# One block in sixteen gets its product by C on VectorE, the others on GpSimd

## The reference

```python
def _L0_ffn_ref(x, A, B, W, bias):          # 64 arrows of rank 16, TOPK = 4
    vecs = jnp.einsum('arh,bsh->bsar', A, x)
    arrows = jnp.linalg.norm(vecs, axis=-1)
    _, idx = jax.lax.top_k(arrows, TOPK)
    routes = jax.nn.one_hot(idx, arrows.shape[-1], dtype=x.dtype).sum(-2) / TOPK
    v = jnp.einsum('bsa,bsar->bsr', routes, vecs)
    delta = jnp.einsum('bsa,ajr,bsr->bsj', routes, B, v)
    return jnp.einsum('bsh,jh->bsj', x, W) + bias + delta

def _L0_attn_ref(x, W_xproj, W_dt, b_dt, A_log, D_param):   # 16 states, rank 128
    xz = jnp.einsum('btd,rd->btr', x, W_xproj)
    delta_r, B_mat, C_mat = ...                              # xz cut in three
    delta = jax.nn.softplus(jnp.einsum('btr,dr->btd', delta_r, W_dt) + b_dt)
    dA = jnp.exp(delta[..., None] * -jnp.exp(A_log))
    Bu = delta[..., None] * B_mat[:, :, None, :] * x[..., None]
    # over time: h = dA_t * h + Bu_t;  y = sum(h * C_t[:, None, :], axis=-1)
    return y + x * D_param

x = x + 0.5 * _L0_ffn_ref(_layernorm(x), A, B, W, bias)
x = x + _L0_attn_ref(_layernorm(x), ...)
x = x + 0.5 * _L0_ffn_ref(_layernorm(x), A, B, W, bias)
```

## Time and profile before

| | |
|---|---|
| median of 3 runs | 2759.53 us (2757.13 to 2759.86) |
| profiled execution | 2758.88 us |
| its span, first to last instruction | 2757.1 us |
| granted TensorE clock, mean | 0.993 |
| PE busy | 94% of the span |
| POOL busy | 85% |
| DVE busy | 81% |
| ACT busy | 54% |

### The profile page before, as it was taken

The page is one execution under the profiler, slowest core; times in us unless marked ns, Lnnn a source line. Parts: engine busy times, 40 slices in busy tenths (PEclk is TensorE's granted clock), DMA queues, the critical chain, the costliest instruction groups (busy, mean ns, idle before and its releaser), DMA issues.

```text
span 2757.1 us, 39894 instructions
## 1 busy us (share of the span) xinstructions
PE 2586.1 (94%) x13593; PEld 1170.8 (42%) x13664; DVE 2219.7 (81%) x2933; ACT 1501.3 (54%) x3363; POOL 2349.9 (85%) x703
## 2 busy tenths in 40 slices
PE   4989999999999999999999999999999999899999
PEld 1444444444434444444444444444444444444444
DVE  7448888888888888888888888888888888888943
ACT  5346667665555655655556555565555555556511
POOL 1138999899989999999999999999999999999910
PEclk9999999999999999999999999999999999999999
DMA  5144544644464545554454445544455445454321
GB/s 217 55 116 152 151 137 141 179 146 139 143 166 143 154 127 155 154 150 143 144 169 137 143 143 170 155 149 133 146 170 151 157 128 156 141 146 153 92 62 54
DMA packets 333217, 390.29 MB, mean 142 GB/s; under 512 B 149459, under 2 KB 249939, under 8 KB 333014
## 3 DMA queue, kind: packets, MB, share of 16 engines
q1 hardware_dynamic: 316118, 354.18, 43.0%
q10 hardware_dynamic: 16896, 33.56, 4.1%
HBM read 250.82 MB, written 103.29 MB: 128 GB/s over the span
## 4 chain that ended last, share of the span: by engine, by line
PE 36%; DVE 34%; ACT 8%; DVEq 7%; issue 7%; DMA 4%; POOL 2%; ACTq 1%; SPq 0%; POOLq 0%
DVE mreg L1154 18%; PE pv L560 12%; PE po L560 7%; PE pv L564 6%; PE po L564 4%; ACT pA L940 3%; PE py L727 3%; DMA delta_scratch<-mreg 2%; DVE pv L1114 2%; DVE sel L1111 2%; DVEq L1119 2%; DVEq L1069 2%; DVE ln_st L1068 1%; DVEq L1113 1%; PE pv L689 1%
## 5 line engine op out<-in xcount | busy, mean ns | idle before, releaser
L528 POOL TENSOR_TENSOR mreg<-mreg 128x2048 f32<-128x2048 f32 x256 | 1161.8, 4538 | 96.8 <-ACT hst L926 92.5
L1154 DVE TENSOR_TENSOR_SCAN mreg<-pA,hst,mreg 128x512 f32<-128x512 f32 (+1 forms) x1024 | 1044.2, 1066 | 76.6 <-ACT pA L940 59.0
L940 ACT ACTIVATE pA<-mreg,nA 128x512 f32<-128x512 f32 (+1 forms) x1280 | 739.7, 597 | 398.3 <-DVE mreg L1154 372.0
L518 POOL TENSOR_TENSOR mreg<-mreg 128x1024 f32<-128x1024 f32 x340 | 794.9, 2362 | 122.3 <-DMA mreg<-delta_scratch 109.7
L560 PE MATMUL pv<-wA,xT 128*128 128x512 f16 x2016 | 458.1, 379 | 28.0 <-DVE xT L1091 26.5
L560 PE MATMUL po<-wW,xT 128*128 128x512 f16 x2016 | 469.6, 380 | 4.0 <-issue 0.5
L560 PE MATMUL po<-wB,uT 128*128 128x512 f16 x2016 | 465.8, 379 | 7.9 <-DVE xin L1077 7.4
L512 POOL TENSOR_TENSOR mreg<-mreg 128x2048 f32<-128x2048 f32 x86 | 389.5, 4529 | 5.5 <-issue 5.2
L560 PEld LDWEIGHTS pv<-wA,xT 128*128 128x128 f16 x2016 | 190.8, 98 | 305.9 <-ACT xT L847 65.8
L560 PEld LDWEIGHTS po<-wB,uT 128*128 128x128 f16 x2016 | 191.3, 98 | 266.3 <-issue 36.4
L560 PEld LDWEIGHTS po<-wW,xT 128*128 128x128 f16 x2016 | 196.0, 98 | 240.1 <-issue 26.3
(11 more groups left out here) (132 smaller groups left out, 2371.7 us busy)
## 6 DMA issues: line engine op xcount, KB each, us to landing
mreg<-delta_scratch SPq DMA_DIRECT2D x256, 512.0 KB, 5.2
mreg<-xnT_scratch SPq DMA_DIRECT2D x128, 256.0 KB, 4.9
delta_scratch<-mreg ACTq DMA_DIRECT2D x128, 256.0 KB
xin<-x SPq DMA_DIRECT2D x32, 512.0 KB, 4.2
x_scratch<-xin SPq DMA_DIRECT2D x32, 512.0 KB, 3.0
xnT_scratch<-auxs SPq DMA_DIRECT2D x32, 512.0 KB, 2.9
yT_scratch<-mreg SPq DMA_DIRECT2D x64, 256.0 KB, 5.6
uT<-yT_scratch SPq DMA_DIRECT2D x32, 512.0 KB, 5.2
```

Of the source, the lines that this page charges most:

```text
L518: pool.tensor_tensor(h[:, half * n:half * n + n, :], u, b.broadcast_to([P, n, c.width]), ALU.mult).then_inc(s_bm, 1)
L528: pool.tensor_tensor(h, h, by_c, ALU.mult).then_inc(s_cm, 1)
L940: last = nc.scalar.activation(dst[:, part, :], src[:, part, :], ACT.Exp, scale=nA[:, m:m + 1])
L1154: last = V.tensor_tensor_scan(h, split(pA[:, i % 2, :], c)[:, part, :], h, before, ALU.mult, ALU.add)
```

## The change

The constant GV = 3 names a group. In every tile the first block of group 3, block i with i % 16 == 12, no longer gets its product by C from GpSimd. VectorE scans that block out of Hr, but writes the states in place over the decays in PSUM (pA) instead of into Hr. After a drain and a wait for C's row it multiplies the states in pA by C's row and writes the product to Hr, where GpSimd's would have been, and gives s_sc behind that. GpSimd's product of group 3 covers the other three blocks. As the states of block 12 are then in pA alone, ScalarE copies their last column to hst from there (`keep_first`, with a drain), ahead of the decay of block 14, which overwrites the buffer. `keep_last` copies the columns of the other three blocks.

```diff
--- before.py
+++ after.py
@@ -11,6 +11,7 @@
 NPR = 3
 NXT = 3
 AHEAD = 10
+GV = 3
 LEAD = 14
 MIX_END = 48
 SCAN0 = 3
@@ -523,8 +524,9 @@
                 c = chunk_of_tile[G // 4]
                 pool.wait_ge(s_sv, G + 1)
                 pool.wait_ge(s_ldc[g], 16 * (c.q + 1))
-                h = split(Hr[:, G % NH, :, :].rearrange("p s t -> p (s t)"), c)
-                by_c = Cr[:, g, 0:c.width].unsqueeze(1).broadcast_to([P, 4 * c.parts, c.width])
+                first = c.parts if g == GV else 0
+                h = split(Hr[:, G % NH, :, :].rearrange("p s t -> p (s t)"), c)[:, first:, :]
+                by_c = Cr[:, g, 0:c.width].unsqueeze(1).broadcast_to([P, 4 * c.parts - first, c.width])
                 pool.tensor_tensor(h, h, by_c, ALU.mult).then_inc(s_cm, 1)
 
             largest(0)
@@ -921,13 +923,25 @@
 
                 act.wait_ge(s_sc, 4 * G + 4)
                 c, k, g = chunk_of_tile[G // 4], channels_at(G // 4), G % 4
-                src = split(Hr[:, G % NH, :, :].rearrange("p s t -> p (s t)"), c)[:, :, c.width - 1]
-                dst = hst[:, 16 * k:16 * (k + c.parts)].rearrange("p (k c) -> p k c", c=16)[:, :, 4 * g:4 * g + 4]
-                nc.scalar.activation(dst, src.rearrange("p (s k) -> p k s", s=4), ACT.Copy).then_inc(s_sv, 1)
+                s0 = 1 if g == GV else 0
+                src = split(Hr[:, G % NH, s0:, :].rearrange("p s t -> p (s t)"), c)[:, :, c.width - 1]
+                dst = hst[:, 16 * k:16 * (k + c.parts)].rearrange("p (k c) -> p k c", c=16)[:, :, 4 * g + s0:4 * g + 4]
+                nc.scalar.activation(dst, src.rearrange("p (s k) -> p k s", s=4 - s0), ACT.Copy).then_inc(s_sv, 1)
+
+            def keep_first(i):
+
+                act.wait_ge(s_sc, i + 1)
+                c, k = chunk_of_tile[i // 16], channels_at(i // 16)
+                src = split(pA[:, i % 2, :], c)[:, :, c.width - 1]
+                dst = hst[:, 16 * k:16 * (k + c.parts)].rearrange("p (k c) -> p k c", c=16)[:, :, i % 16]
+                nc.scalar.activation(dst, src, ACT.Copy)
+                act.drain()
 
             def decay(i):
                 if i % 4 == 1 and i > 4:
                     keep_last(i // 4 - 1)
+                if i % 16 == 4 * GV + 2 and i < 4 * NGRP:
+                    keep_first(i - 2)
                 if i >= 4 * NGRP:
                     return
                 n = i // 16 * 2 + i % 4 // 2
@@ -1150,8 +1164,14 @@
                 for part in range(c.parts):
                     m = column(i, part)
                     h = split(Hr[:, G % NH, s, :], c)[:, part, :]
+                    a = split(pA[:, i % 2, :], c)[:, part, :]
                     before = cst[:, 5:6] if c.fresh else hst[:, m:m + 1]
-                    last = V.tensor_tensor_scan(h, split(pA[:, i % 2, :], c)[:, part, :], h, before, ALU.mult, ALU.add)
+                    last = V.tensor_tensor_scan(a if i % 16 == 4 * GV else h, a, h, before, ALU.mult, ALU.add)
+                if i % 16 == 4 * GV:
+                    dve.drain()
+                    dve.wait_ge(s_ldc[GV], 16 * (c.q + 1))
+                    by_c = Cr[:, GV, 0:c.width].unsqueeze(1).broadcast_to([P, c.parts, c.width])
+                    last = V.tensor_tensor(split(Hr[:, G % NH, s, :], c), split(pA[:, i % 2, :], c), by_c, ALU.mult)
                 last.then_inc(s_sc, 1)
 
             def sum_up(t):
```

## The result

The changed kernel took 2789.46 us, median of 4 runs (2785.42 to 2790.93), against 2759.70 us (2757.13 to 2762.18) of the kernel before: ratio 1.0106, 95% interval 1.0088 to 1.0123. It is slower by 29.8 us; forecast were 24 us and a range of 2757 to 2814.

A forecast was written before the change was run, and what follows sets the result against it. VectorE's work between choice and statistics was taken as the bound, not GpSimd. Terms 20.0 + 1.4 - 1.5 + 1.9 + 2.4 = 24.2 us on 2759.5 gave 2783 us; range for 8 times in 10: 2757 to 2814.

The forecast's parts named there:

- What bounds the kernel: VectorE's work from choice to statistics sets each unit's time; nobody waits for GpSimd, so its 70 us less count 0.
- Prices: Per block: scan into PSUM 0 us extra, DVE product 692 ns plus 75 ns drain; POOL's three-block product 3.45 us.
- the bounds on the scan: In-place scan into PSUM: -0.03 to +0.03 us a block, 2 us either way over 64.
- Exposed ahead of the statistics: Of 32 tiles ahead, 20.0 us from product and drain, 1.4 us from keep_first, less 1.5 us in units with slack.
- not exposed: The one tile ahead of the statistics standing before a load of xin, not among the 26 exposed at 0.77 us.
- Behind the statistics: Of 32 tiles behind, 11 stand ahead of xT's low parts: 7 cost 1.9 us, 4 cost 2.4 us; 0 at the choice.
- What is late next: PE, whose wait for xn grows: On PE, the total wait for xn grows from 62 us to about 85.
- DVE up: VectorE's busy time over the whole run rises by 44 to 49 us.
- xn and xT together up: PE's waits for xn and xT's low part together rise by 15 to 30 us.
- the wait for decays: On DVE: a rise of more than 20 us would show the forecast wrong, with all blocks exposed (that rival: 0.12, 2826 us).
- POOL's idle behind hst: GpSimd's idle behind hst rises by about 90 us.
- the wait for sel: DVE's wait at the squares of the experts' product falls by about 15 us.

The follow-up runs named there:

- GpSimd's relief alone: Kernel before, with GpSimd's product of group 3 covering three blocks and nothing on VectorE in its place: 2759.73 us, ratio 1.0004 to the kernel before.
- the run with matmuls in the waits: Changed kernel plus four unread f16 matmuls on TensorE ahead of its wait for xn in 29 units: 2782.75 us, 1.0083 to the kernel before.
- The run of the 32 behind: Kernel before, changed only in the 32 tiles whose block 12 lies behind its unit's statistics: 2767.97 us, ratio 1.0032 to the kernel before.

## Why the prediction was right

The mechanism held. The size came out right in part by luck: one term was too large, one too small, one was missing, and the errors partly cancel. The profiled executions differ by 30.3 us, and unit by unit that is 15.3 ahead of the statistics, 16.8 behind xn, 0.7 less between the two and 1.2 less ahead of unit 3.

- *What bounds the kernel.* Right. GpSimd's relief alone brought 0.0004 +- 0.0009 of the time, its full load on top of the change cost nothing, and moving a scan across the statistics brought 24 us.
- *Prices.* Scan in PSUM, product, drain and three-block product all came out within 10 ns of their nearest rows; the bounds on the scan (2 us either way) were wide enough.
- *Exposed ahead of the statistics.* Forecast 20.0 + 1.4 - 1.5 = 19.9 us; the units grew by 15.3. Of that difference 2 us are unit 17, where a 2.31 us wait for a load of xin went away, which the term had only as "not exposed"; units 7 and 30 even lost 0.2 to 0.3.
- *Behind the statistics.* Forecast 4.3 us, all in front of xT. Less the share of the clock (below), the units grew by about 11. Four units (4, 12, 20, 28) grew by 1.0 us each where I had counted 0.6. Units 3, 11, 19 and 27, whose block 12 stands at two thirds of the unit, grew by 0.6 and 0.3, which I had counted as free. Unit 24 grew by 1.6 with a longer wait for xT, which the run with matmuls in the waits hadn't. The run of the 32 behind took 8.9 us, about 5 of them with the clock.
- *The term that was missing.* "What is late next: PE, whose wait for xn grows" stopped at the wait's own length and had nothing for the clock. Nine stretches at the lower clock stand against two in the scanning stage. By comparison with runs that have none at the same place, a stretch cost 1.0 to 1.4 us in five units (15, 21, 23, 29, 46), 0.9 and 0.5 in units 53 and 55 and nothing in units 4 and 9, 7.6 us in all; units 25 and 57 gave 1.8 back. That leaves about 6 us, an estimate from the traces, of which the run with matmuls in the waits gave back 4.6.
- *Signs named in advance.* DVE up by 44.4 us (44 to 49 forecast), xn and xT together up by 16.2 (15 to 30), the wait for decays down instead of up by 20. Two were off: POOL's idle behind hst rose by 61 us, not 90, since POOL also waits longer for PE's sums (12.6 to 26.1 us in L519's wait) and for nothing named in front of L513 (5.2 to 33.0 us); and the wait for sel fell by 3 us, not 15. Why so little is not settled; PE reached the squares later too.

## What to carry to other kernels

Ask of a full engine who waits for it before relieving it: here 96% busy was worth nothing, and 85% busy was the bound, in one half of each unit. Where an engine's order alternates between a stretch that the loop runs through and one in which it waits, the place of an instruction decides its price (0.73 against 0.28 us a tile here, with the clock's share in both), and moving work across the border costs nothing and can bring more than removing it elsewhere. A wait of TensorE can cost more than its length. Count the stretches at the lower clock in each trace before you give a difference of a few microseconds to an instruction.

## What the hardware showed unexpectedly

A wait of TensorE of 2.33 us was followed by a short stretch at the lower granted clock, which made the unit 1.3 us longer; with 0.9 us of the wait filled by matmuls that nobody reads, the same place ran at full clock, and the kernel as a whole took 6.7 us less for doing more. Whether a wait is followed by such a stretch can't be told from its length: the same unit with the same 2.55 us had none in one kernel and one in another. How many stretches a kernel has varies too (two and four at the same time of 2760 us). The scan's speed hardly depended on where it writes: 1276 ns in place in PSUM, 1268 into SBUF.
